# Convolution block on single-image PSUM banks, inverse roots on ScalarE, statistics read from PSUM, and one attention loop written out

## The chip, the cores and the metric

The kernel runs on one NeuronCore of a Trainium2 chip. The metric is device time in microseconds (us) from one launch. The kernel before was run three times: median 743.61 us, lowest 742.51, highest 745.41. What can be told from no change here is about 0.5%.

## What is computed

The input is 16 images of 64 channels x 32 x 32, float32. Four blocks follow one another, each as `x = x + block(groupnorm(x))`:

```python
x = x + L0(_gn(x))   # Mamba: projection, 4-tap causal conv, silu, 2-state scan, gate, projection, layer norm
x = x + L1(_gn(x))   # batch norm, 3x3 conv, y = relu(conv) + input, 1x1 conv (64x64) and bias
x = x + L2(_gn(x))   # per image: e1, e2 (32 rows each), softmax(e1^T e2) over 1024 pixels, times asm
x = x + L3(_gn(x))   # bilinear shift per channel, 1x1 conv
```

`_gn` has 32 groups, so two channels share a mean and a variance. L1's batch norm needs a mean and a variance per channel over all 16 images. Both need `(variance + eps)^-0.5`, called a root below.

## The kernel before

All images stay in SBUF in the tile `X`, as 8 pairs: image A of a pair on partitions 0 to 63 (`OF_A`), image B on 64 to 127 (`OF_B`), 1024 pixels in the free dimension, taken in halves of 512 (one PSUM bank). There is no scheduler: each engine's program is written out by hand, and named semaphores tie them together, so the order of the work is the order of the code.

**Roots.** Statistics are gathered on VectorE (`coefs_stat`), summed over a group by a small matmul (`group`), finished on VectorE (`coefs_var`, lines 407 to 412), raised to -0.5 on GpSimd (`power`, line 1174 or 1176), and turned into a shift on VectorE (`coefs_shift`, line 416). This is done ten times: IN_A to IN_D at the start, GN1 and BN1 between L0 and L1, GN2A (pairs 0 to 2) during L1, GN2B (pairs 3 to 7) during attention of pair 0, GN3A and GN3B at the end of attention. Every step of such a chain is an own instruction that waits for the one before it (`link`).

**End of L0.** For each half pair, GpSimd's `output` (L1227, L1228) adds the two states and multiplies with the gate; TensorE's `project_out` (L1429) and `variance` follow; VectorE's `norm` and `residual0` (L542, L547) put the result into `X`. The bank that `project_out` writes is the one that `residual0` of the half before has read.

**L1, the convolution.** For each pair there are two padded planes, `UA` and `UB`. ScalarE's `natural` (L1004) writes image A's normalized pixels on partitions 0 to 63 of `UA` and image B's on 64 to 127 of `UB`. A DMA from SyncE's queue (`shifts`, L352) then copies each plane, one row up, to the other 64 partitions, so that one matmul with 128 rows of weights does two of the three kernel rows. TensorE's `turn1` has nine slots: slots 0 to 2 (`rows01`, L1479 and L1481) and 6 to 8 do two kernel rows at 128 x 64, slots 3 to 5 (`rows2`, L1491) do the third in four 64 x 64 quarters of the array. Bank 0 holds the upper 16 rows of both images, bank 1 the lower 16. VectorE's `relu` (L608) adds the unpadded input `GF`, which GpSimd's `g1` (L1258) writes. At slot 3 of the next pair `pointwise` (L1499) does the 1x1 convolution by two 128 x 128 matmuls with a block-diagonal matrix, and `add1` (L614) adds it to `X`.

From pair 4 on, the operands of the first two attention pairs are made in between (L1534 to the DMAs of `stacked`, L368), and 32 score matmuls (`rows`, L1554) with VectorE's row maxima (L656) are put among the slots of pairs 5 to 7.

**L2, attention.** `attend(p)` has 16 steps; a step has two score matmuls (L1576), two for the maxima of pair p+1 (L1554), and four products (L1587). ScalarE takes the exponentials (L1050), GpSimd adds them up (`sums`, L1289), VectorE takes maxima. At step 2 the operands of pair p+2 are projected (L1534), for which GpSimd has normalized the input (`normed`, L1268). `attend(0)` and `attend(7)` are written out; the six between are a loop of two turns of three on TensorE, ScalarE, VectorE and SyncE; GpSimd's is written out.

```python
            for h in range(2):
                pointwise(7, 1, h)
            t.wait_ge(s["minus_done"], 1)
            t.wait_ge(s["x1_done"], 2 * PAIRS)
            attend(0, 0, lag=False, first=True)
```

## Time and profile before

| | |
|---|---|
| time of the profiled execution | 748.2 us |
| its span, first to last instruction | 746.4 us |
| mean granted TensorE clock | 0.943 of full |
| TensorE matmuls busy | 640.9 us (86%) |
| VectorE busy | 556.5 us (75%) |
| ScalarE busy | 427.5 us (57%) |
| GpSimd busy | 397.8 us (53%) |
| DMA moved | 29.24 MB |

The profiled execution lies 4.6 us above the median of the three timed runs, and its own 1.8 us around the span are launch and end. L0 fills about the first 203 us, the convolution 218 to 325 us, attention 326 to 653 us, and L3 the rest. In the profile's page a busy share is the engine's time with an instruction running; "idle before" is the gap ahead of an instruction, with the one that ended it. PE is TensorE, PEld its weight load, DVE VectorE, ACT ScalarE, POOL GpSimd, SP SyncE.

### The profile page before, as it was taken

Reading aid. Unit: us, or ns where it says so; the run is one execution under the profiler, and the core shown is the slowest. Engines: PE = TensorE matmul, PEld = TensorE weight load, DVE = VectorE, ACT = ScalarE, POOL = GpSimd, SP = SyncE. Lnnn points to the kernel's source line nnn. Section 1 sums busy time; section 2 is a strip of 40 time slices with the busy share of each in tenths; the row PEclk is TensorE's granted clock in tenths of the full one; section 3 lists DMA queues with packets and bytes.
Section 4 is the critical chain, followed back from the end, with each engine's and each line's share of the span. In section 5 each row is a group of like instructions: output and inputs, shape, how many; then the busy total and the mean of one; then the engine's idle time right before and its main releaser. Section 6 shows DMA issues by size and latency. Waiting matters only on the chain.

```text
span 746.4 us, 9091 instructions
## 1 busy us (share of the span) xinstructions
PE 640.9 (86%) x2558; PEld 278.6 (37%) x2558; DVE 556.5 (75%) x886; ACT 427.5 (57%) x726; POOL 397.8 (53%) x252
## 2 busy tenths in 40 slices
PE   4786888887339989989899999999999999858687
PEld 1332333232113332234344344434434343248683
DVE  6996999999423476779769787858788795966546
ACT  2477699898412232045374757557574847675670
POOL 2444787878221230218939696976969596012400
...
DMA packets 14425, 29.24 MB, mean 39 GB/s; under 512 B 4016, under 2 KB 4144, under 8 KB 14256
## 3 DMA queue, kind: packets, MB, share of 16 engines
...
## 4 chain that ended last, share of the span: by engine, by line
PE 39%; DVE 10%; issue 3%; ACT 3%; POOL 2%; DVEq 0%; POOLq 0%; ACTq 0%
PE PS L1587 14%; PE PS L1576 9%; PE PS L1554 6%; DVE SM L656 2%; PE PS L1545 2%; DVE RB L803 2%; PE PS L1605 2%; PE PS L1743 1%; ACT RA L1156 1%; PE PS L1703 1%; DVE RB L312 1%; PE PS L1566 1%; PE PS L1534 1%; PE PS L1714 1%; PE PS L1692 1%
## 5 line engine op out<-in xcount | busy, mean ns | idle before, releaser
L656 DVE TENSOR_REDUCE SM<-PS 128x1 f32<-128x512 f32 x256 | 165.2, 684 | 60.6 <-PE PS L1554 56.5
L1050 ACT ACTIVATE RB<-PS 128x512 f32<-128x512 f32 x256 | 138.9, 594 | 93.6 <-PE PS L1576 92.9
L1289 POOL TENSOR_TENSOR RB<-RB 128x1024 f32<-128x1024 f32 x60 | 141.0, 2369 | 1.8
L1576 PE MATMUL PS<-R 98*128 98x512 f32 x256 | 96.4, 456 | 2.0 <-ACT RB L1050 1.1
L1554 PE MATMUL PS<-R 96*128 96x512 f32 x256 | 89.3, 418 | 8.0 <-DVE SM L656 5.4
L1587 PE MATMUL PS<-RB 128*64 128x512 f32 x320 | 85.4, 616 | 0.0
L1576 PEld LDWEIGHTS PS<-R 98*128 98x128 f32 x256 | 39.4, 192 | 84.8 <-ACT RB L1050 53.8
L1422 PE MATMUL PS<-RA,W 128*128 (+1 forms) x128 | 63.0, 636 | 8.7 <-DVE RB L524 5.3
L1554 PEld LDWEIGHTS PS<-R 96*128 96x128 f32 x256 | 48.7, 192 | 44.0 <-DVE SM L656 26.7
L1289 POOL TENSOR_TENSOR EX<-EX,RB 128x1024 f32<-128x1024 f32 x24 | 56.4, 2371 | 0.8
L1279 POOL TENSOR_TENSOR WS<-RA,WS 128x512 fp32r<-128x512 f32 x14 | 21.8, 1558 | 64.9 <-ACT WS L1034 44.4
L1479 PE MATMUL PS<-RB,WC 128*64 128x512 f32 x96 | 47.8, 621 | 8.8 <-DMA RB<-RB 8.8
L1587 PE MATMUL PS<-RB,RA 128*64 128x512 f32 x192 | 54.5, 647 | 0.0
L1004 ACT ACTIVATE RB<-X,SM 64x1024 f32<-64x1024 f32 x15 | 18.5, 1243 | 62.6 <-PE PS L1481 53.4
L1481 PE MATMUL PS<-RB,WC 128*64 128x512 f32 x96 | 47.8, 621 | 0.0
L1422 PEld LDWEIGHTS PS<-RA,W 128*128 128x128 f32 x128 | 24.5, 201 | 46.0 <-issue 27.5
L524 DVE TENSOR_TENSOR_SCAN RB<-RB,PS 128x512 f32<-128x512 f32 x32 | 38.3, 1238 | 0.6
L1258 POOL TENSOR_SCALAR RB<-X,SM 128x1024 f32<-128x1024 f32 x8 | 10.1, 1265 | 50.4 <-DVE RB L608 49.1
L1056 ACT ACTIVATE R<-PS 2x512 fp32r<-2x512 f32 x32 | 17.1, 581 | 33.7 <-PE PS L1566 33.7
L1176 POOL TENSOR_TENSOR SM<-SM 128x2 f32<-128x2 f32 (+5 forms) x9 | 8.6, 951 | 47.3 <-DVE SM L412 47.3
L448 DVE SCALAR_TENSOR_TENSOR RB<-PS,W,RB 128x1023 f32<-128x1023 f32 (+2 forms) x24 | 30.6, 1280 | 2.3 <-ACT RB L882 1.6
L1227 POOL TENSOR_TENSOR EX<-RB 128x512 f32<-128x512 f32 x16 | 20.4, 1275 | 22.1 <-DVE RB L536 22.1
...
## 6 DMA issues: line engine op xcount, KB each, us to landing
...
RB<-RB SPq DMA_DIRECT2D x16, 280.5 KB, 3.1
...
```

The lines of the kernel that those rows point to most:

```text
L448: i = v.scalar_tensor_tensor(AC[b][:, j:L], xp[:, 0:L - j], col("cw%d" % (3 - j)), AC[b][:, j:L], ALU.mult, ALU.add)
L524: i = v.tensor_tensor_scan(tB[h][j], tA[h][j], bank(1 + j), first, ALU.mult, ALU.add)
L656: v.tensor_reduce(MX[:, par, tile, h:h + 1], bank(2 + h), AX.X, ALU.max)\
L1050: act(slot[:, h * HALF:(h + 1) * HALF], bank(4 + h), ACT.Exp).then_inc(s["p_ready"], 1)
L1279: g.tensor_tensor(zl[:, cols], EF[h], zh[:, cols], ALU.subtract).then_inc(s["lo_done"], 1)
L1289: i = g.tensor_tensor(out, out, PT[j % SLOTS][par], ALU.add)
L1422: i = mm(bank(1 + 2 * o + j), mat("bc%d" % (2 * o + j)), half(XS, p, h))
L1479: mm(conv_out(OF_A, h), WC[:, dx, :], UA[b][:, y, dx:dx + WW], start=(h == 0 and dx == 0), stop=(h == 1 and dx == 2))
L1481: return mm(conv_out(OF_B, h), WC[:, 3 + dx, :], UB[b][:, y, dx:dx + WW], start=(h == 0 and dx == 0), stop=(h == 1 and dx == 2))
L1554: mm(bank(2 + h), stack(b, par, 0)[0:96, tile * P:(tile + 1) * P], stack(b, par, 1)[0:96, h * HALF:(h + 1) * HALF]).then_inc(s["s_mm"], 1)
L1576: mm(bank(4 + h), stack(b, par, 1)[0:98, j * P:(j + 1) * P], stack(b, par, 0)[0:98, h * HALF:(h + 1) * HALF]).then_inc(s["t_mm"], 1)
L1587: i = mm(PS[par * C:(par + 1) * C, h, :], V[b][:, j, par * C:(par + 1) * C], PT[j % SLOTS][par][:, h * HALF:(h + 1) * HALF], start=(j == 0 ...
```

## The change

It has six parts.

1. Roots from GN1 on are two ScalarE instructions (`root`: Ln, then Exp with scale -0.5) in place of GpSimd's power. The four at the start keep GpSimd. A root stands in ScalarE's program where its result is needed: behind `natural` of pair 4, at step 15 of `attend(0)`, step 5 of `attend(7)`, and ahead of a transpose copy at the end.
2. `coefs_var` and its batch-norm twin read the group sums where the matmul left them in PSUM, in three instructions for four; the batch-norm chain has fewer steps. GN2B's `coefs_shift` moves behind `attend(0)`, and GpSimd's `normed(3)`, which waits for it, from step 6 of its sums to behind step 7.
3. The very last `output` of L0 is done on VectorE (`output_last`).
4. Each convolution bank now holds one image: partitions 0 to 63 its upper 16 rows, 64 to 127 its lower 16. `relu` needs its second input in that layout, so `g1` writes a scratch tile `GI` and four DMAs per pair (`moves`, on SyncE's queue) bring it into `GF`. The shifts of the planes are issued from ScalarE's queue, behind both `natural` of the pair. `pointwise` is four 64 x 64 matmuls on the four quarters of the array in place of two 128 x 128.
5. The first pair's convolution uses only unshifted planes: nine taps, each four 64 x 64 matmuls, and both banks end at the ninth.
6. `pointwise` of pair 7 moves into step 0 of `attend(0)`, into banks 0 and 1, and VectorE's adds and statistics of pair 7 into its steps 1 to 6. VectorE's attention loop is written out.

```diff
+        GI = [TMP[:, b * L:(b + 1) * L] for b in range(2)]
         GF = [TMP[:, (2 + b) * L:(3 + b) * L] for b in range(2)]
         YF = [TMP[:, (4 + b) * L:(5 + b) * L] for b in range(2)]
...
+            def moves(p):
+                b = p % 2
+                sp.wait_ge(s["g1_ready"], p + 1)
+                need(sp, s["y1_done"], 2 * p - 2)
+                for k, of in enumerate((OF_A, OF_B)):
+                    dst = GF[b][:, k * HALF:(k + 1) * HALF]
+                    for h in range(2):
+                        sp.dma_start(dst[h * C:(h + 1) * C, :], GI[b][of, h * HALF:(h + 1) * HALF])\
+                            .then_inc(s["moved_odd" if b else "moved_even"], 16)
...
             for p in range(6):
-                shifts(p)
+                moves(p)
             stacked(0, 0)
-            shifts(6)
-            shifts(7)
+            for p in (6, 7):
+                moves(p)
...
-                link(v.tensor_copy(GS[:, lo:hi].rearrange("p a b -> p (a b)"), PS[:, 7, 0:2 * (hi - lo)]))
-                link(v.tensor_tensor(SQ[:, lo:hi], GS[:, lo:hi, 0], GS[:, lo:hi, 0], ALU.mult))
-                link(v.tensor_tensor(VAR[:, lo:hi], GS[:, lo:hi, 1], SQ[:, lo:hi], ALU.subtract))
-                v.tensor_scalar(VAR[:, lo:hi], VAR[:, lo:hi], EPS, None, ALU.add).then_inc(s["var_ready"], 1)
+                both = PS[:, 7, 0:2 * (hi - lo)].rearrange("p (a b) -> p a b", b=2)
+                link(v.tensor_copy(GS[:, lo:hi, 0], both[:, :, 0]))
+                link(v.tensor_tensor(SQ[:, lo:hi], both[:, :, 0], GS[:, lo:hi, 0], ALU.mult))
+                v.scalar_tensor_tensor(VAR[:, lo:hi], both[:, :, 1], EPS, SQ[:, lo:hi], ALU.add, ALU.subtract)\
+                    .then_inc(s["var_ready"], 1)
...
+            def output_last():
+                v.wait_ge(s["hc_done"], 2 * PAIRS)
+                v.wait_ge(s["o_mm"], 2 * PAIRS - 2)
+                link(v.tensor_tensor(tY[1], tA[1][0], tA[1][1], ALU.add))
+                v.tensor_tensor(tY[1], tY[1], half(ZS, PAIRS - 1, 1), ALU.mult).then_inc(s["y_last"], 1)
...
                 skip(p, h)
+                if tail:
+                    output_last()
                 if lead:
                     soft(p + 1, h)
...
+            b0, b1 = BM[:, 0, :], BM[:, 1, :]
+            link(v.tensor_tensor(MV, MV, SC.unsqueeze(2).to_broadcast([P, PAIRS, 2]), ALU.mult))
+            v.tensor_tensor(b1, MV[:, :, 1], SC, ALU.mult)
+            link(v.tensor_tensor(b0, MV[:, :, 0], SH, ALU.add))
+            link(v.tensor_tensor(SQ, b0, MV[:, :, 0], ALU.add))
+            link(v.tensor_tensor(SQ, SQ, SH, ALU.mult))
             link(v.tensor_tensor(b1, b1, SQ, ALU.add))
             v.tensor_reduce(BS, BM, AX.X, ALU.add).then_inc(s["stat_ready"], 1)
+            mean, msq = PS[:, 7, 0:1], PS[:, 7, 1:2]
+            link(v.tensor_copy(BT[:, 0:1], mean))
+            link(v.tensor_tensor(BT[:, 2:3], mean, BT[:, 0:1], ALU.mult))
+            v.scalar_tensor_tensor(BT[:, 3:4], msq, EPS, BT[:, 2:3], ALU.add, ALU.subtract)\
+                .then_inc(s["var_ready"], 1)
+            link(v.tensor_scalar(SHG, SH, BT[:, 0:1], col("gamma"), ALU.subtract, ALU.mult))
+            v.wait_ge(s["root_done"], BN1 + 1 - GN1)
+            v.tensor_scalar(SB, SC, BT[:, 4:5], col("gamma"), ALU.mult, ALU.mult)
+            v.tensor_scalar(TB, SHG, BT[:, 4:5], col("beta"), ALU.mult, ALU.add).then_inc(s["coef_ready"], 1)
...
+            def end7(h):
+                v.wait_ge(s["x1_done"], 2 * PAIRS - 1 + h)
+                return stats(7, h)
+            attend(0, 0, lag=False, v0=7, extra={1: lambda: add_half(7, 0, 0), 2: lambda: add_half(7, 1, 0),
+                                                 3: lambda: end7(0), 6: lambda: link(end7(1)),
+                                                 8: lambda: coefs_stat(3, PAIRS),
+                                                 13: lambda: coefs_var(GN2B, 3, PAIRS)})
+            coefs_shift(GN2B, 3, PAIRS)
+            for p in range(1, PAIRS - 1):
+                attend(p, p % 3)
...
+            def root(nth, lo=0, hi=PAIRS):
+                a.wait_ge(s["var_ready"], nth + 1)
+                src, dst = (BT[:, 3:4], BT[:, 4:5]) if nth == BN1 else (VAR[:, lo:hi], SC[:, lo:hi])
+                link(act(dst, src, ACT.Ln))
+                act(dst, dst, ACT.Exp, scale=-0.5).then_inc(s["root_done"], 1)
...
                 natural(p, UA, OF_A, "ua_done")
                 natural(p, UB, OF_B, "ub_done")
+                shifts(p)
+                if p == 4:
+                    root(GN2A, 0, 3)
...
+            def conv_out(k, h):
+                return PS[h * C:(h + 1) * C, k, :].rearrange("p (y x) -> p y x", y=BAND)
+            def rows01(p, k, dx):
+                u = (UA, UB)[k][p % 2]
+                for h in range(2):
+                    y = slice(h * BAND, (h + 1) * BAND)
+                    i = mm(conv_out(k, h), WC[:, 3 * k + dx, :], u[:, y, dx:dx + WW],
+                           start=(k == 0 and dx == 0), stop=(k == 1 and dx == 2))
+                return i
             def rows2(p, dx):
-                b = p % 2
-                for of, u in ((OF_A, UA), (OF_B, UB)):
+                for k, (u, of) in enumerate(((UA, OF_A), (UB, OF_B))):
                     for h in range(2):
-                        k = (OF_A, OF_B)[h]
-                        y = h * BAND + 2 - (k is not of)
-                        i = mm(conv_out(of, h), WC[k, 6 + dx, :], u[b][k, y:y + BAND, dx:dx + WW],
-                               start=(h == 1 and dx == 0), stop=(h == 0 and dx == 2))
+                        y = h * BAND + 2
+                        i = mm(conv_out(k, h), WC[of, 6 + dx, :], u[p % 2][of, y:y + BAND, dx:dx + WW],
+                               start=(k == 1 and dx == 0), stop=(k == 0 and dx == 2))
                 return i
-            def pointwise(p, b, h):
-                t.wait_ge(s["y1_done"], 2 * p + h + 1)
-                need(t, s["x1_done"], 2 * p + h - 1)
-                mm(bank(4 + h), mat("w11"), YF[b][:, h * HALF:(h + 1) * HALF]).then_inc(s["w1_mm"], 1)
+            def first_pair(tap):
+                for k, (u, of) in enumerate(((UA, OF_A), (UB, OF_B))):
+                    dy, dx = divmod(tap, 3)
+                    at = tap if dy == 2 else 3 * ((dy + k) % 2) + dx
+                    for h in range(2):
+                        y = h * BAND + dy
+                        i = mm(conv_out(k, h), WC[of, at, :], u[0][of, y:y + BAND, dx:dx + WW],
+                               start=(tap == 0), stop=(tap == 8))
+                    if tap == 8:
+                        i.then_inc(s["conv_mm"], 1)
+            def pointwise(p, b, first=4):
+                t.wait_ge(s["y1_done"], 2 * p + 2)
+                need(t, s["x1_done"], 2 * p)
+                for h, rows in enumerate((OF_A, OF_B)):
+                    for k in range(2):
+                        i = mm(PS[k * C:(k + 1) * C, first + h, :], mat("w11")[rows, h * C:(h + 1) * C],
+                               YF[b][rows, k * HALF:(k + 1) * HALF])
+                    i.then_inc(s["w1_mm"], 1)
...
+                t.wait_ge(s["shifted_odd" if p % 2 else "shifted_even"], 32 * (p // 2) + 32 * (p % 2))
                 for k in range(SLOTS1):
                     if k == 3 and p:
-                        pointwise(p - 1, (p - 1) % 2, 0)
-                        pointwise(p - 1, (p - 1) % 2, 1)
+                        pointwise(p - 1, (p - 1) % 2)
...
+                        if n == 0 and first:
+                            pointwise(7, 1, 0)
...
-                    if j == 5 and p == 0:
-                        power(GN2B, 3, PAIRS)
-                    if j == 6 and p == 0:
+                    if j == 7 and p == 0:
...
-            for p in range(PAIRS):
+            t.wait_ge(s["ua_done"], 1)
+            t.wait_ge(s["ub_first"], 1)
+            for tap in range(9):
+                first_pair(tap)
+            for p in range(1, PAIRS):
                 turn1(p, extras.get(p, {}))
-            for h in range(2):
-                pointwise(7, 1, h)
             t.wait_ge(s["minus_done"], 1)
-            t.wait_ge(s["x1_done"], 2 * PAIRS)
+            t.wait_ge(s["x1_done"], 2 * PAIRS - 2)
             attend(0, 0, lag=False, first=True)
```

TensorE, from the last slot of the convolution into `attend(0)`. Before (L1479 and L1481 are the last slot, L1499 the 1x1 convolution of pair 7, L1576 scores, L1554 scores for the maxima, L1566 the maxima as matmul rows):

```order
L1479 MATMUL PS<-RB,WC 64x512
L1481 MATMUL PS<-RB,WC 64x512
L1499 MATMUL PS<-RB,W 128x512 [waits x1_done,y1_done] x2
L1576 MATMUL PS<-R 128x512 [waits m_copied,x1_done,minus_done]
L1576 MATMUL PS<-R 128x512
L1554 MATMUL PS<-R 128x512 [waits s_read,stack_in]
L1554 MATMUL PS<-R 128x512 [waits s_read]
L1566 MATMUL PS<-IB,MB 2x128 [waits m_copied,m_ready]
```

After, the same place (L1513 is the last slot, L1622 scores, L1600 scores for the maxima, L1544 the 1x1 convolution, L1612 the maxima):

```order
L1513 MATMUL PS<-RB,WC 64x512 x2
L1622 MATMUL PS<-R 128x512 [waits m_copied,x1_done,minus_done]
L1622 MATMUL PS<-R 128x512
L1600 MATMUL PS<-R 128x512 [waits s_read,stack_in]
L1600 MATMUL PS<-R 128x512 [waits s_read]
L1544 MATMUL PS<-RB,W 64x512 [waits x1_done,y1_done]
L1544 MATMUL PS<-RB,W 64x512 x3
L1612 MATMUL PS<-IB,MB 2x128 [waits m_copied,m_ready]
```

The 1x1 convolution stands behind the first scores and asks for `y1_done`; the first scores no longer ask for the last add of pair 7 (the waits have the same names, the counts of `x1_done` are 16 and 14).

VectorE, from step 13 of `attend(0)` to the loop. Before (L409 to L412 are GN2B's `coefs_var`, L656 maxima, L663 to L667 `both_parts`, L416 its `coefs_shift`):

```order
L409 COPY SM<-PS 128x10 [waits group_mm]
L410 TENSOR_TENSOR SM<-SM 128x5 [waits dve_step]
L411 TENSOR_TENSOR SM<-SM 128x5 [waits dve_step]
L412 TENSOR_SCALAR SM<-SM 128x5 [waits dve_step]
L656 TENSOR_REDUCE SM<-PS 128x1 [waits s_mm] x2
L663 TENSOR_REDUCE SM<-SM 128x8 [waits mrow_mm,s_read]
L664 TENSOR_REDUCE MB<-SM 128x8
L665 TENSOR_REDUCE SM<-MB 128x8 [waits dve_step]
L667 TENSOR_REDUCE MB<-SM 128x8 [waits dve_step]
L656 TENSOR_REDUCE SM<-PS 128x1 [waits s_mm] x2
L416 SCALAR_TENSOR_TENSOR SM<-SM 128x5 [waits pow_done]
L656 TENSOR_REDUCE SM<-PS 128x1 [waits s_mm,coef_ready]
```

After (L408 to L410 are `coefs_var`, L666 maxima, L673 to L677 `both_parts`, L418 `coefs_shift`):

```order
L408 COPY SM<-PS 128x5 [waits group_mm]
L409 TENSOR_TENSOR SM<-PS,SM 128x5 [waits dve_step]
L410 SCALAR_TENSOR_TENSOR SM<-PS,SM 128x5 [waits dve_step]
L666 TENSOR_REDUCE SM<-PS 128x1 [waits s_mm] x2
L673 TENSOR_REDUCE SM<-SM 128x8 [waits mrow_mm,s_read]
L674 TENSOR_REDUCE MB<-SM 128x8
L675 TENSOR_REDUCE SM<-MB 128x8 [waits dve_step]
L677 TENSOR_REDUCE MB<-SM 128x8 [waits dve_step]
L666 TENSOR_REDUCE SM<-PS 128x1 [waits s_mm] x4
...
L418 SCALAR_TENSOR_TENSOR SM<-SM 128x5 [waits root_done]
L666 TENSOR_REDUCE SM<-PS 128x1 [waits s_mm,coef_ready]
L666 TENSOR_REDUCE SM<-PS 128x1 [waits s_mm] x7
```

Two instructions of the chain read PS in place of SM, the last is gone, and the shift stands behind all maxima of the pair, straight ahead of those of the next; the branch that followed is gone.

ScalarE, ahead of the first operands for attention. Before (L1004 is `natural`, L1018 and L1022 the operands of pair 0):

```order
L1004 ACTIVATE RB<-X,SM 64x32x32 x2
L1004 ACTIVATE RB<-X,SM 64x32x32 [waits conv_mm] x8
L1018 ACTIVATE RA<-PS,SM 128x512 [waits z_mm]
L1022 ACTIVATE PS<-PS,SM 128x512
```

After (L1037 is `natural`, L1031 the shift DMAs, L969 and L970 the root GN2A, L1054 and L1058 the operands, L1070 their high parts; the rows begin behind the DMAs of pair 4):

```order
L969 ACTIVATE SM<-SM 128x3 [waits var_ready]
L970 ACTIVATE SM<-SM 128x3 [waits act_step]
L1037 ACTIVATE RB<-X,SM 64x32x32 [waits conv_mm] x2
L1031 DMA RB<-RB 64x1122 [waits ua_done]
L1031 DMA RB<-RB 64x1122 [waits ub_done]
L1054 ACTIVATE RA<-PS,SM 128x512 [waits z_mm]
L1058 ACTIVATE PS<-PS,SM 128x512
L1054 ACTIVATE RA<-PS,SM 128x512 [waits z_mm]
L1058 ACTIVATE PS<-PS,SM 128x512
L1070 ACTIVATE R<-RA 128x512 [waits zf_done] x2
L1037 ACTIVATE RB<-X,SM 64x32x32 [waits conv_mm] x2
L1031 DMA RB<-RB 64x1122 [waits ua_done]
```

The DMAs stand among ScalarE's instructions, and those of pair 6 now come before the operands of attention pair 1; before, they stood in SyncE's queue behind the twelve DMAs of the first stack.

## Rows read from the trace of the kernel before

**Rows 1.** the page's part 4, the chain by engine.

```profile
PE 39%; DVE 10%; issue 3%; ACT 3%; POOL 2%; DVEq 0%; POOLq 0%; ACTq 0%
```

**Rows 2.** timeline, 190 to 218 us: start, us, engine, line, operation, [idle before <-releaser].

```profile
190.20 0.75 DVE L536 SCALAR_TENSOR_TENSOR RB<-RA,W,RB 128x512 f32<-128x512 f32 x1
...
191.90 0.75 DVE L547 SCALAR_TENSOR_TENSOR X<-PS,W,X 128x512 f32<-128x512 f32 x1
...
193.70 2.08 PE L1429 MATMUL PS<-EX,W 128*128 128x512 f32 x2 [3.96 <-POOL EX L1228]
...
202.84 0.18 DVE L575 TENSOR_TENSOR SM<-SM 128x16 f32<-128x16 f32 x1 [1.40 <-ACT RB L960]
...
204.79 1.65 POOL L1176 TENSOR_TENSOR SM<-SM 128x8 f32<-128x8 f32 x1 [10.46 <-DVE SM L412]
...
209.94 0.57 POOL L1174 TENSOR_TENSOR SM<-SM 128x1 f32<-128x1 f32 x1 [3.51 <-DVE SM L593]
...
211.79 3.64 ACT L1004 ACTIVATE RB<-X,SM 64x1024 f32<-64x1024 f32 x3 [8.98 <-DVE SM L599]
...
217.92 1.08 PE L1479 MATMUL PS<-RB,WC 128*64 128x512 f32 x1 [8.83 <-DMA RB<-RB]
```

**Rows 3.** timeline, ScalarE, the first microseconds.

```profile
4.65 0.20 ACT L874 ACTIVATE SM<-W 128x2 f32<-128x2 f32 x1 [2.65 <-DMA W<-pack]
```

**Rows 4.** timeline, TensorE, slots of pair 6.

```profile
292.89 1.98 PE L1499 MATMUL PS<-RB,W 128*128 128x512 f32 x4
294.80 1.09 PE L1534 MATMUL PS<-RA,WE 64*64 64x512 f32 x8
295.82 0.73 PE L1554 MATMUL PS<-R 96*128 96x512 f32 x2
```

**Rows 5.** timeline, TensorE's first score matmul for attention.

```profile
277.86 0.73 PE L1554 MATMUL PS<-R 96*128 96x512 f32 x2 [2.13 <-DMA R<-R]
```

**Rows 6.** the page's part 6, plane shifts: KB each, median us to landing.

```profile
RB<-RB SPq DMA_DIRECT2D x16, 280.5 KB, 3.1
```

**Rows 7.** busy time by windows: PE, PEld, DVE, ACT, POOL, then PEclk, DMA share, GB/s.

```profile
275.70:277.90 2.20, 0.07 (x2) 0.04 (x1) 2.17 (x4) 0.00 (x0) 0.00 (x0) 1.00 0.96 215
364.00:374.50 10.50, 10.50 (x36) 4.96 (x35) 4.24 (x10) 4.31 (x8) 10.29 (x6) 0.51 0.00 0
497.00:500.50 3.50, 3.41 (x7) 1.31 (x8) 1.42 (x3) 0.14 (x1) 2.22 (x2) 0.55 0.00 0
```

**Rows 8.** timeline, start and end of attend(0).

```profile
323.13 2.26 PE L1499 MATMUL PS<-RB,W 128*128 128x512 f32 x4
...
326.28 0.70 PE L1576 MATMUL PS<-R 98*128 98x512 f32 x2 [0.89 <-POOL R L1304]
...
342.19 19.00 POOL L1289 TENSOR_TENSOR RB<-RB 128x1024 f32<-128x1024 f32 x8
...
349.88 0.69 DVE L634 TENSOR_TENSOR PS<-PS,W 128x512 f32<-128x512 f32 x1
...
357.11 1.78 DVE L410 TENSOR_TENSOR SM<-SM 128x5 f32<-128x5 f32 x1
358.93 2.28 DVE L411 TENSOR_TENSOR SM<-SM 128x5 f32<-128x5 f32 x1
...
362.06 1.10 PE L1554 MATMUL PS<-R 96*128 96x512 f32 x2 [2.48 <-DVE SM L656]
...
367.49 1.20 POOL L1268 TENSOR_SCALAR RB<-X,SM 128x1024 f32<-128x1024 f32 x1
...
377.31 1.09 PE L1534 MATMUL PS<-RB,WE 64*64 64x512 f32 x8
```

**Rows 9.** timeline, the turn of the attention loop.

```profile
495.75 2.67 DVE L656 TENSOR_REDUCE SM<-PS 128x1 f32<-128x512 f32 x4 [3.18 <-issue]
496.49 1.20 PE L1554 MATMUL PS<-R 96*128 96x512 f32 x2 [1.42 <-DVE SM L656]
497.62 1.98 PE L1587 MATMUL PS<-RB,RA 128*64 128x512 f32 x4
```

128 lines of the change are left out of this document (48 added, 80 removed).

## The prediction, made before the changed kernel was run

> **What bounds the kernel now.** I read the page first. Its chain of waits is led by TensorE with 39% [rows 1], and the table of busy times says why: matmuls run for 86% of the span. So the question for each edit is whether it takes time off TensorE's stream, or off a stretch in which TensorE stands still. The timeline between the blocks shows such a stretch: from 193.70 us, the last projection of L0, to 217.92, the first convolution matmul, TensorE has five short pieces of work, and all else is a chain through VectorE, GpSimd, ScalarE and a DMA [rows 2]. The view of waits inside the convolution has one long gap of TensorE: 2.13 us on the DMAs of the first attention operands [rows 5]. Windows then give the granted clock, which the other views hide: it is 1.00 in most of attention, but about half (1.2 GHz in place of 2.4) in 364 to 374.5 us and 497 to 500.5 us, each time behind a gap of TensorE, of 2.48 and 1.42 us [rows 7, 8, 9]. Behind the gap of 0.89 us at 326.28 no matmul is slow [rows 8]. So a gap of TensorE costs itself, and if it is as long as 1.4 us, several microseconds at half speed behind it.
>
> **Start, four roots.** One VectorE instruction of about 0.2 us less in each. Only the first stands alone on the path, the others lie between VectorE's own work, so 0.2 to 0.8 us; I take 0.5.
>
> **Last gate on VectorE.** GpSimd's add and multiply lie between the end of L536 (190.20 + 0.75 = 190.95) and the projection at 193.70 [rows 2]. On VectorE the two take about 0.71 each, but stand ahead of `norm` and `residual0` of the half before, and the projection needs the bank that `residual0` frees. From 190.95: 1.42 for the gate, 0.72 and 0.77 for the other two, is 193.86, and the projection starts at about 193.9. No gain, a loss of 0.2. Before, L547 was done at 192.65, well ahead [rows 2].
>
> **Roots GN1 and BN1.** The chain runs from 202.84 to 211.79 [rows 2]. VectorE has 25 instructions in it and then 17 (`SHG` hides behind the root); they follow one another every 0.2 us, so 8 less is 1.5, one of them being half hidden. GpSimd's powers take 1.65 and 0.57 [rows 2]. A small ScalarE instruction took 0.20 [rows 3], so Ln, Exp and the handover are 0.45 to 0.5 twice; gained 1.4. Together 2.9.
>
> **First pair without shifted planes.** From 211.79 ScalarE writes planes at 1.21 us each (3.64 for three), and TensorE begins at 217.92, when the shifted planes have landed [rows 2]. Now it begins when the first plane is written, 1.3 us after the coefficients: 4.8 gained. The matmul time of the pair stays nine slots. But both banks end with the ninth tap, and the next pair's first slot waits for the relu of bank 0: handover and 0.69, about 0.9 lost. Net 3.9. The shifted planes of pair 1 are written by 213.1 + 2.4 on the old clock and land some 4 us on, well before the nine slots are over.
>
> **1x1 convolution on quarters.** The two full matmuls of a pair take 1.91 us (292.89 to 294.80). Right behind stand four 64 x 64 matmuls of the same width, and they take 1.02 (to 295.82) [rows 4]. So 0.89 per pair, 7 pairs inside the slots: 6.2. Bounds: nothing, if the quarters did not overlap, and 7 x 1.0. In pairs 6 and 7 VectorE's maxima stand close behind, and short waits for them will grow; I take off 0.6, so 5.6.
>
> **The first stack.** TensorE waits 2.13 us for it [rows 5]. The way from L1534 to the landing is the same, but TensorE has one 1x1 convolution less work in it, 0.9 more wait. Besides, the planes of pair 6 were shifted behind the stack in one queue; now ScalarE issues them as soon as they are written, in the middle of it. They are 2 x 280.5 KB [rows 6], and the DMA engines are already 0.96 busy at 215 GB/s there [rows 7]: 2.6 us at that rate, of which I count 1.8. Bounds 0 and 2.6. Sum: 2.7 lost. The clock falls behind this gap before and after. The Trainium skill (DMA: Bandwidth & Descriptors, Rules for kernel authors) says that spreading DMAs over issuing engines brings no bandwidth, since all run on the same 16 DMA engines and interleave. The window above agrees as far as it shows one queue filling them; by the rule the delay would be the full 2.6.
>
> **Start and end of `attend(0)`.** Three things cost TensorE here [rows 8, 7]. It starts 3.15 us after the convolution (323.13 to 326.28), for the 1x1 convolution and the adds of pair 7; now four quarters (1.0) lie in step 0: 2.1 gained. VectorE's two instructions L410 and L411 take 1.78 and 2.28 us, where such ones take 0.18 [rows 2]; both run beside GpSimd's unbroken adds (19.00 us for eight). They make TensorE wait 2.48. The new ones read PSUM, as L634 does, which takes its usual 0.69 beside the same adds; then VectorE is 3.7 less late and the gap goes. The 10.5 us at clock 0.51 that follow go with it: 5.2. Sum 9.8. The Trainium skill (SBUF — State Buffer, Who interferes with whom) says that a VectorE instruction with two SBUF inputs contends with a GpSimd instruction that reads SBUF, and one with at most one does not; L410 and L411 agree. It speaks against the moved `coefs_shift`, which has two SBUF inputs and now stands ahead of the maxima of pair 1: by the rule it can be held for a whole GpSimd add.
> What is late next is GpSimd. `normed(3)` (1.20 us) ran after ten adds, now after all twelve. Its adds start some 2 us earlier than at 342.19, 17.1 after the convolution's end; twelve at 2.37 are 28.5; with the 1.2 it is ready 46.8 after it. TensorE came to L1534 at 54.2 (377.31 - 323.13) and without its 9.8 comes at 44.4 to 45. So it waits about 2.0, and by what gaps did before, half clock for 3.5 us follows, 1.8 more. With 0.4 for the shift: 9.8 - 2.0 - 1.8 - 0.4 = 5.6 gained. Bounds 3 and 9.8.
>
> **Loop written out.** At the turn VectorE stands still 3.18 us with nothing to wait for; TensorE waits 1.42 of it, and 3.5 us at clock 0.55 follow [rows 9, 7], 1.8. ScalarE's and TensorE's own branches stay, and were no later than their work. Gain 3.2; bounds 0, if another branch is as late, and 3.6. The other loop turns of attention are bound by TensorE and stay.
>
> **The end.** GN3A's root is needed long after. GN3B's goes to ScalarE, but ahead of the work that ScalarE does before the last `normed3`, so 0; bounds 0.3 both ways.
>
> **Sum.** 0.5 - 0.2 + 2.9 + 3.9 + 5.6 - 2.7 + 5.6 + 3.2 - 0 = 18.8. The profiled execution took 748.2 us (span 746.4 and 1.8 around), so 729.4 in one like it; the median of the runs shown is 4.6 lower: 743.6 - 18.8 = 724.8 us.
>
> **Rivals.**
> *More is gained:* the wait for `normed(3)` stays under 1.4 us, the clock stays up, and the shifts of pair 6 find room between the stack's transfers. Gains 3.0 and 1.8 more: 720. For it: the estimates of both are sums of small steps, each uncertain by a microsecond.
> *VectorE is too full in `attend(0)`:* it now also does the adds and statistics of pair 7 in steps 1 to 6, some 2.8 us, and had little pause before. If it falls behind by a step there, TensorE gets gaps again, and the clock falls: only 1 of the 5.6 is left: 729.5. Against: the same work stood right before step 0, and 3.7 us of stalls go.
> *The quarters do not overlap, or ScalarE's queue is slow:* 1x1 convolution without gain: 730.4. Against: [rows 4].
> *Slower: TensorE waits for shifted planes in every pair.* Both `natural` of pair p start when the convolution of p-2 ends; 2.5 us later ScalarE issues two DMAs, about 1 us; landing takes 3.1 [rows 6], and up to 1 us more beside the four `moves` (512 KB): 7.6 us. Before, the first shift went off 1.2 us sooner and nothing ran beside it. A slot is 0.87 to 1.0 us (four quarters, [rows 4]), so a pair of nine and the 1x1 convolution takes TensorE at least 8.7. So 1.1 us are left. From a landing at 10.1 on, the gap is 1.4, and with half clock behind it costs 3.2 a pair, six times 19: that eats the gain. At 10.6 us it is 22: 747 us, slower. Issuing from ScalarE, and the load of a second stream, are not in this trace; but they would have to be 2.5 to 3 us worse.
>
> **How the numbers follow.** A measurement of this kernel can tell about 0.5%, 3.7 us, from no change. Forecast 0.55, more gained 0.17, VectorE too full 0.12, quarters or queue 0.10, slower 0.06 (two thirds of it beyond 747, one third between). The range 717 to 733 holds the first four and leaves out the slower case and the far ends. Faster 0.94, same 0.02, slower 0.04.
>
> **What would show it.** L1544 should take 1.0 us per pair, where L1499 took 1.9. The first convolution matmul should begin at 210 us (0.5 + 2.9 + 4.8 - 0.2 before 217.92). TensorE's gap for the first stack should be 4 to 6 us. VectorE's L409 and L410 in `attend(0)` should take 0.2. No "issue" gap on VectorE near the middle of attention. TensorE should wait for GpSimd's `normed(3)` at its second L1580 of attention. I am wrong if a shift (L1031) is waited for beyond pair 1, or if the granted clock is low in the convolution other than at its start and behind the stack.

## The result and the profile after

The changed kernel took 732.98 us (median of 4 executions, 732.48 to 735.11), the kernel before 744.51 beside it (4 executions, 742.51 to 745.6). The ratio is 0.985 with a 95% interval of 0.981 to 0.988: faster by 11.5 us. The forecast was 724.8 us, a gain of 18.8. The measured median lies inside the range of 717 to 733 by 0.02 us, which is luck: it is 8.2 us above the forecast, and a second profile of the changed kernel (e11 below) took 735.9 us. The profiled execution took 732.5 us (span 730.7).

Start of the convolution, in the timeline of the changed kernel; it answers to [rows 2] (L549 is `residual0`, L969 and L970 a root, L1037 `natural`, L1533 the first pair's taps, L1513 `rows01`).

```profile
192.66 2.05 PE L1462 MATMUL PS<-EX,W 128*128 128x512 f32 x2 [4.19 <-DVE X L549]
...
203.25 0.21 ACT L969 ACTIVATE SM<-SM 128x8 f32<-128x8 f32 x1 [1.51 <-DVE SM L410]
203.49 0.21 ACT L970 ACTIVATE SM<-SM 128x8 f32<-128x8 f32 x1
...
207.57 3.65 ACT L1037 ACTIVATE RB<-X,SM 64x1024 f32<-64x1024 f32 x3 [0.69 <-DVE SM L606]
209.06 9.78 PE L1533 MATMUL PS<-RB,WC 64*64 64x512 f32 x72 [3.23 <-ACT RB L1037]
...
219.78 2.80 PE L1513 MATMUL PS<-RB,WC 128*64 128x512 f32 x12 [0.94 <-DVE RB L614]
```

The last projection waits for `residual0` (L549). From it to the start of the first plane is 14.91 us where it was 18.09, so the chain gave 3.2. The first matmul starts 1.49 us behind that, not 6.13. The last projection itself starts 1.0 us earlier, so the convolution starts 8.9 us earlier; TensorE then waits 0.94 us for the relu behind the pair's last tap.

The convolution itself, same view (L1544 is the 1x1 convolution; L1600 are early scores), and the windows behind its two gaps. In a windows line the number behind the five engines' busy times is the granted clock, as in [rows 7]; 0.50 is 1.2 GHz, called half clock here. L1622 is the first score matmul of `attend(0)`, right behind the last slot of the convolution.

```profile
231.40 1.09 PE L1544 MATMUL PS<-RB,W 64*64 64x512 f32 x8
...
240.29 1.09 PE L1544 MATMUL PS<-RB,W 64*64 64x512 f32 x8
...
267.44 1.22 PE L1600 MATMUL PS<-R 96*128 96x512 f32 x2 [4.46 <-DMA R<-R]
...
307.24 0.50 PE L1600 MATMUL PS<-R 96*128 96x512 f32 x1 [1.53 <-DVE SM L666]
...
316.76 0.72 PE L1622 MATMUL PS<-R 98*128 98x512 f32 x2
```

```profile
267.50:277.50 10.00, 10.00 (x33) 2.51 (x33) 3.98 (x6) 0.00 (x0) 0.00 (x0) 0.50 0.13 29
308.50:311.50 3.00, 3.00 (x13) 0.59 (x9) 0.69 (x1) 0.00 (x0) 0.00 (x0) 0.50 0.00 0
```

The 1x1 convolution takes 1.09 us where it took 1.98, and a pair comes every 8.89 us. But the stack is waited for 4.46 us, and TensorE then runs 10 us at half clock (1.2 GHz). In pair 7 a second gap of 1.53 us has 3 us at half clock behind it. Before, the same wait was of 1.07 us, and the clock stayed at 1.00:

```profile
315.14 0.49 PE L1554 MATMUL PS<-R 96*128 96x512 f32 x1 [1.07 <-DVE SM L656]
```

The whole convolution, from its first matmul to the end of its last slot, lasts 107.7 us (209.06 to 316.76), where it lasted 105.2 (217.92 to 323.13 in [rows 2, 8]): longer, although 6.2 us of matmuls (7 x 0.89) are gone from it.

The first attention pair, same view; it answers to [rows 8].

```profile
333.63 28.61 POOL L1325 TENSOR_TENSOR RB<-RB 128x1024 f32<-128x1024 f32 x12
...
333.91 1.09 PE L1600 MATMUL PS<-R 96*128 96x512 f32 x2 [0.69 <-DVE SM L666]
...
336.18 2.13 DVE L402 TENSOR_TENSOR SM<-SM 128x5 f32<-128x5 f32 x1
...
350.88 0.16 DVE L409 TENSOR_TENSOR SM<-PS,SM 128x5 f32<-128x5 f32 x1
351.07 0.16 DVE L410 SCALAR_TENSOR_TENSOR SM<-PS,SM 128x5 f32<-128x5 f32 x1
...
358.21 1.73 DVE L418 SCALAR_TENSOR_TENSOR SM<-SM 128x5 f32<-128x5 f32 x1
...
362.34 1.20 POOL L1304 TENSOR_SCALAR RB<-X,SM 128x1024 f32<-128x1024 f32 x1
363.78 0.72 PE L1600 MATMUL PS<-R 96*128 96x512 f32 x2 [0.29 <-POOL RB L1304]
364.43 1.09 PE L1580 MATMUL PS<-RB,WE 64*64 64x512 f32 x8
```

The two instructions that read PSUM take 0.16 us, beside the same GpSimd adds that held L410 and L411 for 1.78 and 2.28 [rows 8]; the gap of 2.48 us is gone. L402 and L418, with two SBUF inputs, took 2.13 and 1.73. The Trainium skill (SBUF — State Buffer, Who interferes with whom) says that a VectorE instruction with two SBUF inputs contends with a GpSimd instruction that reads SBUF, and one with at most one such input, outside its two-port modes, does not. These rows agree, though the wait is not there each time (L403, with two SBUF inputs too, took 0.17 right behind L402). GpSimd's `normed(3)` ends at 363.54, and TensorE goes on right behind it. From the end of the convolution's last slot to L1580 it is 47.67 us, where it was 54.18. From there to the same line of pair 4 (484.97) it is 120.54 us, where it was 123.90.

### The profile page after: what moved, and what is told of

The parts are those of the page before. It is cut to its first block, busy times and chain, and to the rows that moved or that the text cites. A ratio compares the mean times of both kernels' runs of the same rounds, so it can differ in the third digit from the quotient of the medians.

```text
span 730.7 us, 8928 instructions
## 1 busy us (share of the span) xinstructions
PE 631.9 (86%) x2614; PEld 275.5 (38%) x2614; DVE 550.1 (75%) x873; ACT 429.9 (59%) x738; POOL 389.6 (53%) x244
## 4 chain that ended last, share of the span: by engine, by line
PE 58%; DVE 19%; issue 8%; ACT 6%; POOL 6%; DMA 1%; SPq 1%; POOLq 0%; DVEq 0%; ACTq 0%
PE PS L1635 15%; PE PS L1622 10%; PE PS L1600 9%; PE PS L1513 5%; DVE RB L450 3%; PE PS L1522 3%; PE PS L1591 2%; DVE RB L816 2%; DVE SM L430 2%; PE PS L1653 2%; DVE RB L526 2%; DVE PS L518 2%; PE PS L1795 1%; DVE RB L533 1%; PE PS L1533 1%
## 5 line engine op out<-in xcount | busy, mean ns | idle before, releaser
L666 DVE TENSOR_REDUCE SM<-PS 128x1 f32<-128x512 f32 x256 | 165.0, 684 | 60.9 <-PE PS L1600 60.4
L1622 PE MATMUL PS<-R 98*128 98x512 f32 x256 | 95.6, 452 | 1.3 <-ACT RB L1086 1.3
L1600 PE MATMUL PS<-R 96*128 96x512 f32 x256 | 88.9, 418 | 8.5 <-DMA R<-R 4.5
L1622 PEld LDWEIGHTS PS<-R 98*128 98x128 f32 x256 | 38.9, 189 | 82.6 <-ACT RB L1086 56.2
L1600 PEld LDWEIGHTS PS<-R 96*128 96x128 f32 x256 | 48.4, 192 | 45.4 <-DVE SM L666 22.8
L1635 PE MATMUL PS<-RB,RA 128*64 128x512 f32 x192 | 52.0, 620 | 0.0
L1037 ACT ACTIVATE RB<-X,SM 64x1024 f32<-64x1024 f32 x15 | 18.5, 1242 | 45.3 <-PE PS L1513 36.8
L1513 PE MATMUL PS<-RB,WC 128*64 128x512 f32 x168 | 41.7, 613 | 0.9 <-DVE RB L614 0.9
L430 DVE BATCH_NORM_STATS2 SM<-X 128x6 f32<-128x512 f32 x48 | 31.5, 684 | 1.8 <-DMA X<-x 1.4
L1257 POOL TENSOR_TENSOR RB<-RB 128x512 f32<-128x512 f32 x16 | 20.3, 1272 | 16.1 <-ACT RB L942 16.0
L1468 PE MATMUL PS<-RB,W 128*128 128x512 f32 x32 | 19.0, 676 | 11.4 <-ACT RB L956 11.4
```

The source lines that it names most:

```text
L430: return v.bn_stats(BST[:, p, h, :], half(X, p, h))
L666: v.tensor_reduce(MX[:, par, tile, h:h + 1], bank(2 + h), AX.X, ALU.max)\
L1513: i = mm(conv_out(k, h), WC[:, 3 * k + dx, :], u[:, y, dx:dx + WW], start=(k == 0 and dx == 0), stop=(k == 1 and dx == 2))
L1600: mm(bank(2 + h), stack(b, par, 0)[0:96, tile * P:(tile + 1) * P], stack(b, par, 1)[0:96, h * HALF:(h + 1) * HALF]).then_inc(s["s_mm"], 1)
L1622: mm(bank(4 + h), stack(b, par, 1)[0:98, j * P:(j + 1) * P], stack(b, par, 0)[0:98, h * HALF:(h + 1) * HALF]).then_inc(s["t_mm"], 1)
L1635: i = mm(PS[par * C:(par + 1) * C, h, :], V[b][:, j, par * C:(par + 1) * C], PT[j % SLOTS][par][:, h * HALF:(h + 1) * HALF], start=(j == 0 ...
```

## The experiments

All times are medians, but for e1 and e11, which are one execution each; a ratio is to the kernel before in the same set of runs, with its 95% interval. "Better" and "worse" compare with the 732.98 us of the changed kernel, which was run in another set: the kernel before took 744.5 to 744.9 us in each set, and such a difference is uncertain by 2 to 4 us. Five executions of the changed kernel took 732.5 to 735.9 us. Every execution of e2, e3, e8 and e9 was shorter than all five, every one of e5 and e6 longer; e4 and e7 overlap with them. The roots on ScalarE, the first pair on unshifted planes and the operands in PSUM have no experiment of their own; for them there are the rows above alone.

**e1_before_again**, the kernel before, unchanged, one profile.

> The kernel before, unchanged, profiled once more. Its first profiled execution took 748.2 us, its timed runs 742.5 to 745.6, so the two traces differ by 15.7 us where the medians differ by 11.5. Theory A: the first profile had a stretch at half clock that most executions don't have, most likely the 10.5 us behind the gap at 359.6 us; then this profile is near 744 us and the half-clock stretch there is 3 to 4 us long. Theory B: profiling itself costs the kernel before more; then this one is near 748 us again with the same windows at half clock.

744.15 us, span 742.4. Its timeline, and its windows behind the gap in the first attention pair and at the turn of the loop:

```profile
323.36 2.26 PE L1499 MATMUL PS<-RB,W 128*128 128x512 f32 x4
...
362.31 1.10 PE L1554 MATMUL PS<-R 96*128 96x512 f32 x2 [2.49 <-DVE SM L656]
...
374.49 1.09 PE L1534 MATMUL PS<-RB,WE 64*64 64x512 f32 x8
...
493.65 1.09 PE L1554 MATMUL PS<-R 96*128 96x512 f32 x2 [1.36 <-DVE SM L656]
```

```profile
364.00:367.40 3.40, 3.40 (x14) 1.89 (x12) 1.41 (x4) 2.08 (x4) 3.40 (x2) 0.50 0.00 0
369.00:372.00 3.00, 3.00 (x19) 1.56 (x18) 1.54 (x4) 1.97 (x4) 3.00 (x2) 1.00 0.00 0
494.00:497.50 3.50, 3.40 (x18) 1.27 (x17) 2.29 (x5) 1.08 (x2) 2.45 (x2) 1.00 0.00 0
```

Expectation A held. These gaps are the same as in [rows 8, 9] within 0.1 us, the half clock behind them is not: about 3.4 us where [rows 7] has 10.5, and none at the turn. The first profile was of a costlier execution, and two terms of the sum had its clock in them. Pair 0 of attention takes 51.13 us here (323.36 to 374.49) and the stretch to the same line of pair 4 122.32. The wait for the first stack is 2.69 us here, 2.13 in [rows 5]. From this execution to the changed kernel's the spans differ by 11.7 us, as the medians do. So it is the better one to count against, though still one execution.

**e2_shift6_behind**, the plane shifts of pair 6 back behind the first stack in SyncE's queue.

```diff
 (SyncE)      stacked(0, 0)
+             plane_shifts(6)
              for p in (6, 7):
                  moves(p)
 (ScalarE)    natural(p, UB, OF_B, "ub_done")
-             shifts(p)
+             if p == 7:
+                 shifts(p)
```

> The changed kernel, but the plane shifts of pair 6 go back into SyncE's queue behind the first stack, as before. Theory gap-and-clock: the shifts in the middle of the stack lengthened TensorE's gap for it (2.13 before, 4.46 after, of which 0.9 is the shorter 1x1 convolution). Then the gap is 3.0 to 3.4 us here, the half-clock stretch behind it shorter than the 10.2 us of the changed kernel, and the kernel 1.2 to 4 us faster than the changed one (729 to 732 us). Rival: the twelve stack transfers are bound by their own issue, and the gap grew since TensorE came earlier; then the gap stays at 4.3 to 4.5 and the time at 733.

728.47 us, ratio 0.979 (0.975 to 0.983): 4.5 us better than the changed kernel.

```profile
265.07 0.73 PE L1611 MATMUL PS<-R 96*128 96x512 f32 x2 [2.34 <-DMA R<-R]
```

```profile
265.10:268.50 3.40, 3.40 (x20) 1.05 (x20) 2.64 (x5) 0.00 (x0) 0.00 (x0) 1.00 0.97 237
```

The gap is 2.1 us shorter (4.46 to 2.34), so the shifts in the middle of the stack cost that, and no half clock is behind it. The rival, a gap that stays at 4.3 to 4.5 us, is out. But this is the profile of the fastest of four executions (725.4, 726.0, 730.9 and 731.5 us, mean clocks 0.958, 0.955, 0.953 and 0.951), and the slower two may well have half clock here. Between the two profiles lie 7.1 us (spans 730.7 and 723.6): 2.1 of gap and 5.1 for 10.2 us at half clock.

**e3_late_fills**, the early scores of pair 5 from slot 7 on, four in place of seven, the others in pairs 6 and 7.

```diff
-        FILLS = {5: (3, 7), 6: (0, 12), 7: (0, 13)}
+        FILLS = {5: (7, 4), 6: (0, 14), 7: (0, 14)}
```

> The changed kernel, but the score matmuls for attention pair 0 begin at slot 7 of pair 5 in place of slot 3 (counts 4, 14, 14 in pairs 5, 6, 7 in place of 7, 12, 13), so TensorE has four more slots, 3.6 us, of convolution before it needs the first stack. Theory gap-and-clock: the gap of 4.46 falls to about 0.9, no half-clock stretch follows (10.2 us at half, 5.1 lost), and the kernel is 6 to 8.6 us faster than the changed one: 724 to 727 us. Rival, VectorE bounds the last pairs: the fuller pairs 6 and 7 give it back in gaps for the maxima, with half clock behind them: less than 3 us gained, 730 us or more.

729.32 us, ratio 0.979 (0.977 to 0.982).

```profile
269.06 0.73 PE L1600 MATMUL PS<-R 96*128 96x512 f32 x2 [0.89 <-DMA R<-R]
...
299.71 0.72 PE L1600 MATMUL PS<-R 96*128 96x512 f32 x1 [1.73 <-DVE SM L666]
...
356.51 0.73 PE L1600 MATMUL PS<-R 96*128 96x512 f32 x2 [2.40 <-POOL RB L1304]
```

The gap at the stack is 3.6 us shorter and the clock stays up. It gained 3.7 us, between the theory's 6 to 8.6 and the rival's less than 3: pair 7 is more crowded on VectorE (1.73 us), and TensorE, now early, waits 2.40 us for `normed(3)`.

**e4_loop_back**, the changed kernel with VectorE's loop of two turns again.

```diff
-            for p in range(1, PAIRS - 1):
-                attend(p, p % 3)
+            with v.Fori(0, 2) as k:
+                ch.enter(k, 3 * 6)
+                for c in range(3):
+                    attend(3 * k + c + 1, (c + 1) % 3)
+                ch.leave(2)
```

> The changed kernel with VectorE's attention loop as a loop again. My term was 3.2 us: VectorE's gap of 3.2 us at the turn returns, TensorE waits about 1.4 us and runs 3.5 us at half clock: 736 us. Rival: what the traces show at the turn is a difference of the two executions' clocks and not of the loop; then the time stays at 733 within 1.5.

736.51 us, ratio 0.988 (0.985 to 0.992): 3.5 us worse, as the theory gave. Its profile has the gap, but not the half clock behind it:

```profile
487.46 1.10 PE L1603 MATMUL PS<-R 96*128 96x512 f32 x2 [1.21 <-DVE SM L666]
```

```profile
487.50:491.00 3.50, 3.40 (x14) 1.41 (x18) 2.29 (x4) 1.65 (x4) 2.92 (x2) 1.00 0.00 0
```

**e12_before_unrolled** is the reverse edit, on the kernel before.

> The kernel before with VectorE's attention loop written out and nothing else. Theory A, by the second profile of the kernel before, in which the turn of the loop has TensorE's gap of 1.36 us and no half clock behind it: 1.4 us gained, 743.1. Rival B, by the first profile, where 3.5 us at half clock follow the gap: 3.2 gained, 741.3, about what e4_loop_back lost (3.5). By both TensorE has no gap at about 493 us.

741.98 us against 744.77, ratio 0.997 (0.995 to 1.000), between the two expectations. Its profile has no gap at the turn. From L1531 of pair 0 to that of pair 4 it takes 120.40 us (371.79 to 492.19), 1.9 less than in e1_before_again. The medians say 2.8 and 3.5, with 2 us or more of uncertainty each. The traces say 1.9, or 3.5 against the first profile; on the changed kernel 1.5 (124.45 us in e4, 122.97 in e11, both with 6.8 us at half clock behind the wait for `normed(3)`). So it hangs on the clock: of the four profiles with the turn's gap (1.2 to 1.4 us) the first one and e10 have 3.4 us at half clock behind it, e1 and e4 none. The edit is worth 1.5 to 1.9 us where the clock stays up and about 3.5 where it would fall.

**e5_full_pointwise**, two 128 x 128 matmuls for the 1x1 convolution.

```diff
-                for h, rows in enumerate((OF_A, OF_B)):
-                    for k in range(2):
-                        i = mm(PS[k * C:(k + 1) * C, first + h, :], mat("w11")[rows, h * C:(h + 1) * C],
-                               YF[b][rows, k * HALF:(k + 1) * HALF])
+                for h in range(2):
+                    i = mm(bank(first + h), mat("w11"), YF[b][:, h * HALF:(h + 1) * HALF])
                     i.then_inc(s["w1_mm"], 1)
```

> The changed kernel with the 1x1 convolution as two 128 x 128 matmuls a pair in place of four 64 x 64 on quarters of the array (the banks then hold a product of the mixed layout, so x is not the block's value; number and size of all other instructions are the same). Theory A, the quarters run two at a time and TensorE's stream bounds the convolution: 0.89 us more in each of 8 pairs, 7.1 in all, 739 to 741 us against 733.0. Rival B, in pairs 5 to 7 and in the first attention pair VectorE's maxima bound the stretch anyway, so only pairs 1 to 4 gain: 3.6 us, 736 to 737. In the profile the line of the 1x1 convolution takes 1.9 to 2.0 us a pair by both.

738.68 us (ratio 0.991, 0.989 to 0.994), 5.7 worse than the changed kernel (5.1 by the ratios): between the two theories, and near to what the sum had (5.6). In the profile the line takes 1.98 us a pair, and the pairs come every 9.95 us, 1.06 more than above:

```profile
231.81 1.98 PE L1543 MATMUL PS<-RB,W 128*128 128x512 f32 x4
...
241.76 1.98 PE L1543 MATMUL PS<-RB,W 128*128 128x512 f32 x4
```

**e6_pointwise7_ahead**, the 1x1 convolution, adds and statistics of pair 7 back between convolution and attention.

```diff
-            t.wait_ge(s["x1_done"], 2 * PAIRS - 2)
+            pointwise(7, 1)
+            t.wait_ge(s["x1_done"], 2 * PAIRS)
             attend(0, 0, lag=False, first=True)
...
-            attend(0, 0, lag=False, v0=7, extra={1: lambda: add_half(7, 0, 0), 2: lambda: add_half(7, 1, 0),
-                                                 3: lambda: end7(0), 6: lambda: link(end7(1)),
-                                                 8: lambda: coefs_stat(3, PAIRS),
+            link(add1(7, 1))
+            attend(0, 0, lag=False, v0=7, extra={8: lambda: coefs_stat(3, PAIRS),
```

> The changed kernel with the 1x1 convolution, the adds and the statistics of pair 7 back between the convolution and the first attention pair. Theory A, as predicted: TensorE stands outside its stream for about 1.0 us of matmul and 2.1 for relu and adds, of which 2.1 net is lost: 735 us. Rival B: that work on VectorE in steps 1 to 6 is what makes the 0.69 us gap at 333.91 us and the 3.4 us at half clock behind it (1.7 lost), so ahead of the pair it costs no more than inside: 732.5 to 733.5. In the profile the first score matmul of attention starts 2 to 3 us later after the last convolution matmul by both; only by B does TensorE run without a gap and at full clock through the first pair.

738.87 us (ratio 0.993, 0.991 to 0.996), 5.9 worse, more than either theory gave.

```profile
316.67 1.09 PE L1538 MATMUL PS<-RB,W 64*64 64x512 f32 x8 [1.12 <-issue]
...
319.25 0.73 PE L1616 MATMUL PS<-R 98*128 98x512 f32 x2 [1.49 <-DVE X L620]
...
367.08 0.72 PE L1594 MATMUL PS<-R 96*128 96x512 f32 x2 [2.72 <-POOL RB L1298]
```

```profile
320.50:327.20 6.70, 6.70 (x25) 3.43 (x24) 3.88 (x7) 3.92 (x8) 0.00 (x0) 0.51 0.01 2
```

The two gaps of 1.12 and 1.49 us bring 6.7 us at half clock, 3.4 us lost, which the move avoids. The prediction gave it 2.1, since in the kernel before the clock stayed up at this place [rows 8]. The gap of 0.69 us at 333.91 is gone, so rival B names a real cause, but a cheap one.

**e7_normed3_earlier**, `normed(3)` behind step 6 of GpSimd's adds, its shift at step 15.

```diff
-            coefs_shift(GN2B, 3, PAIRS)
+                                                 15: lambda: coefs_shift(GN2B, 3, PAIRS)})
...
-                    if j == 7 and p == 0:
+                    if j == 6 and p == 0:
```

(ScalarE's root moves from step 15 to 14.)

> The changed kernel with the shift of GN2B at step 15 of the first attention pair on VectorE, its root at step 14 on ScalarE, and GpSimd's normed(3) behind step 6 of its adds in place of behind step 7. Theory A: TensorE's wait for normed(3), 0.29 us in the profile of the changed kernel but 2.4 us with half clock behind it in two others of nearly the same kernel, goes in every execution: 729 to 732 us. Rival B: the shift, with two SBUF inputs, is held beside GpSimd's adds for 1.8 to 2.3 us as L410 and L411 were before, makes the maxima behind it late, and TensorE gets that gap in place of the other: 733 to 736.

731.89 us (ratio 0.984, 0.979 to 0.988). No wait for `normed(3)` is left, the shift took 0.35 us (1.87 in e8, where no gap follows it either), and no gap follows. The gain of 1.1 us is within the uncertainty. In the profile, pair 0 still has the stretch at half clock behind the gap of 0.69 us.

**e11_after_again**, the changed kernel, one more profile.

> The changed kernel once more, for the stretches at half clock that change from one execution to the next. Theory A: the 10.2 us at half clock behind the stack gap (267.4 us) and the 3.4 us in pair 7 are there again, since the gaps that go ahead of them are in the order of the work; what may differ is the stretch at 335.7 us in the first attention pair, and where it is absent TensorE waits 2.4 us for normed(3) at 363.8 in place of 0.29: span 729 to 733. Rival B: the long stretch was peculiar to the first profile: span 726 to 728.

735.92 us, span 734.1, just above what theory A gave. Timeline and windows:

```profile
270.57 0.83 PE L1600 MATMUL PS<-R 96*128 96x512 f32 x2 [4.47 <-DMA R<-R]
...
363.82 1.21 PE L1600 MATMUL PS<-R 96*128 96x512 f32 x2 [2.38 <-POOL RB L1304]
```

```profile
270.90:274.20 3.30, 3.30 (x15) 0.82 (x17) 1.41 (x3) 0.00 (x0) 0.00 (x0) 0.53 0.31 69
364.00:370.00 6.00, 6.00 (x17) 1.94 (x18) 1.29 (x2) 1.71 (x3) 0.75 (x1) 0.50 0.00 0
335.80:339.00 3.20, 3.20 (x18) 1.76 (x16) 3.13 (x9) 1.08 (x2) 3.12 (x3) 1.00 0.89 205
```

Theory A held for pair 0: without the half clock at 336 us TensorE is early, waits 2.38 us for `normed(3)` and pays at least 6 us at half clock behind it. So GpSimd bounds this pair, and whether TensorE is slow ahead of it or waits at it changes little. For the stack it was half wrong: the gap is the same to 0.01 us, but the half clock behind it was short, some 3.4 us. Behind nearly the same gap (4.5 to 4.6 us) it lasted 10 us in e4, e6 and e7, and 5 us in e5. Here the convolution lasts 105.2 us up to the end of its last slot, 2.5 less than in the first profile of the same kernel.

**e9_spread_only**: the early scores by slot, none ahead of slot 5 of pair 5, few in slots 3 to 6 of pairs 6 and 7. **e10_before_spread**: the same table in the kernel before.

```diff
-        FILLS = {5: (3, 7), 6: (0, 12), 7: (0, 13)}
+        FILLS = {5: (0, 0, 0, 0, 0, 1, 1, 2, 2), 6: (2, 2, 2, 1, 1, 0, 1, 2, 2), 7: (2, 2, 2, 1, 1, 0, 1, 2, 2)}
```

> The changed kernel with one edit of e8_together alone: the 32 early score matmuls given slot by slot (none ahead of slot 5 of pair 5, none or one in slots 3 to 6 of pairs 6 and 7); the plane shifts of pair 6 stay on ScalarE's queue in the middle of the first stack. Theory A, most of what e8_together gained beyond the changed kernel (15.5 us) is TensorE's gaps for the stack and in pair 7 with the half clock behind them, and they go by the places of these matmuls alone: 719 to 723 us. Rival B, without room between the stack's transfers the gap comes back as 2 us at slot 5, and with it the half clock: 725 to 729.

> The kernel before with the same table of places for the 32 early score matmuls and nothing else. Theory A, the convolution before had only 2.1 us of stack gap with 3.4 us at half clock behind it and 1.1 us in pair 7 with none: 2.1 + 1.7 + about 1 are there to be gained, 739 to 741 us against 744.5. Rival B, its TensorE stream is 0.9 us a pair longer and already covers what the table would cover, and the matmuls moved out of pair 5 crowd pairs 6 and 7: 743 to 746.

e9 took 726.7 us (ratio 0.976, 0.973 to 0.979), as rival B gave: pair 7 has no gap of over 0.35 us left, but

```profile
268.69 0.71 PE L1600 MATMUL PS<-R 96*128 96x512 f32 x1 [2.73 <-DMA R<-R]
...
357.33 1.04 PE L1600 MATMUL PS<-R 96*128 96x512 f32 x2 [2.38 <-POOL RB L1304]
```

```profile
268.70:275.40 6.70, 6.70 (x18) 1.88 (x20) 2.69 (x5) 0.00 (x0) 0.00 (x0) 0.51 0.20 45
357.40:360.70 3.30, 3.30 (x12) 0.83 (x14) 1.29 (x2) 0.30 (x1) 0.86 (x1) 0.52 0.00 0
```

e10 took 740.47 us against 744.77 (ratio 0.995, 0.993 to 0.998), as theory A gave: the kernel before had 3.4 (by the ratio) to 4.3 us to gain by this table, the changed one 6.3.

**e8_together**: the edits of e2, e9 and e7 in one kernel.

> The changed kernel with four edits: the plane shifts of pair 6 in SyncE's queue behind the first stack, the 32 early score matmuls of the convolution given slot by slot (none ahead of slot 5 of pair 5, so that the stack has landed, and one or none in slots 3 to 6 of pairs 6 and 7, where VectorE is busy with the adds and statistics), and normed(3) one step earlier. Theory A, gaps of TensorE and the half clock behind them are what is left of the convolution's cost: the stack gap goes wholly (728.5 of the first edit alone less 2.3), the gap of 1.5 to 1.7 in pair 7 and its half clock (3.3) go, and 0.5 for normed(3): 722 to 725 us. Rival B: VectorE has 27 maxima, four adds and the relus in two pairs and is the bound there however they are spread, so the gap only moves: 726 to 728.

717.47 us (716.13 to 720.23), ratio 0.964 (0.960 to 0.968): 15.5 us better than the changed kernel and better than either theory. Its stack gap, and its windows over the stretch from the first convolution matmul to the end of attention:

```profile
266.35 0.50 PE L1611 MATMUL PS<-R 96*128 96x512 f32 x1 [0.61 <-DMA R<-R]
```

```profile
210.00:618.00 408.00, 403.29 (x1886) 160.90 (x1886) 313.70 (x539) 231.21 (x408) 251.83 (x129) 1.00 0.24 56
```

In 408 us TensorE stands still 4.7, and from 214 us on it never leaves 2.4 GHz. Against e9 alone it is 9.2 us: 2.1 of stack gap and 6.7 us at half clock behind it (3.4), 2.4 of wait for `normed(3)` with 3.3 us at half clock behind it (1.7), 9.6 in sum. My expectation of 722 to 725 had left out the last two, since the profile I wrote it from had them as a wait of 0.29 us.

## Why the prediction was off

Direction and most mechanisms were right, the size was not, and that the median still lies in the range is luck. Counted against e1_before_again, whose distance to the changed kernel's first profile is that of the medians, the steps come out so (us gained). The prediction put TensorE at L1580 46.8 us behind the convolution's end, 7.4 earlier than before, and 1.8 at half clock behind it:

| step | predicted | measured |
|---|---|---|
| start, gate, roots, first pair's first matmul | 8.0 | 8.5 (217.59 to 209.06) |
| convolution, first matmul to the end of its last slot | 2.0 | -1.9 (105.77 to 107.70) |
| from there to L1580 in `attend(0)` | 7.4 | 3.5 (51.13 to 47.67) |
| from there to L1580 of pair 4, with the loop's turn | 1.4 (3.2 less 1.8) | 1.8 (122.32 to 120.54) |
| the rest | 0 | -0.2 |
| sum | 18.8 | 11.7 |

The measured column is one execution of each kernel. With e11 for the changed kernel it reads 5.9, 0.6, 3.0, -0.7 and -0.6, 8.2 in sum: a row can move by 2 to 3 us from one execution to the next.

**Right.** The chain gave 3.2 (predicted 2.9). The last gate on VectorE moved the wait to `residual0`, as reckoned. The first pair gained 4.6 at its start and lost 0.94 at its end (4.8 and 0.9). The quarters run two at a time: 0.89 us a pair, and 5.7 in all by e5 (5.6). The PSUM operands freed L409 and L410 from GpSimd's adds. TensorE was to reach L1580 46.8 us behind the end of the convolution, bound by `normed(3)`; `normed(3)` ended 46.8 us behind it (363.54 - 316.76). The wait of 2.0 us there and the half clock behind it came in e11 (2.38 us, at least 6 us at half clock), and not in the first profile (0.29 us and none), where TensorE was late by the half clock at 336 us. None of the slower rival's waits came: no shift (L1031) was waited for. One of the prediction's own signs of being wrong did come, half clock in the convolution other than at its start and behind the stack: in pair 7.

**A term that was mis-sized: the first stack.** "Sum: 2.7 lost. The clock falls behind this gap before and after." The gap was about right: 2.3 us longer than in the first profile and 1.8 than in e1, and by e2 2.1 us of it are the shifts of pair 6 amid the stack (1.8 was my value; the 2.6 of full interference was too much). Wrong was that the half clock behind costs the same before and after. Behind 2.1 to 2.7 us it lasted 3.4 in the three profiles of the kernel before (the first, e1, e12), behind 4.5 to 4.6 us 10 in four of the six that have this gap: 3.4 us more lost. In e11 it was no more than before. e2 gives 4.5 us in the median for 2.1 of gap. The prediction priced the clock wherever a gap would go, and not where one grew.

**The step that was missing: pair 7.** "Short waits for them will grow; I take off 0.6." One of them grew from 1.07 to 1.53 us and so fell among those with half clock behind (1.5 us of time): with the growth about 2.0. In e5, with 0.9 us more work on TensorE, it was 1.08 and nothing followed. e9 took the gap away.

**The largest part: terms read from one execution.** "The 10.5 us at clock 0.51 that follow go with it: 5.2", and 1.8 at the turn of the loop. In e1_before_again the same gaps cost 1.7 and nothing. The pair of first profiles shows 6.5 and 3.4 for the two steps, 9.9 in all, and the forecast had 8.8. But a median isn't an execution like that one: 748.2 us stood 4.6 above it, and the forecast subtracted this 4.6 from the start and kept the gain that was part of it. Against e1 the two steps give 5.2, 4.6 less than against the first profile.

What stays open is why the half clock behind the same 4.5 us gap lasts 10 us in one execution and 3.4 in another, and why gaps of 0.7 us in pair 0 have it behind them in some (the changed kernel, e2, e7) and not in others (e3, e4, e5, e8, e9, e11).
